# Routed experts with fp32r products in three terms instead of full-precision products

## The reference, cut to what matters

```python
def _ffn(x, w1, w2, w3):
    return jax.nn.silu(x @ w1.T) * (x @ w3.T) @ w2.T
for i in range(sw1.shape[0]):                 # 2 shared experts, over all 2048 rows
    shared = shared + _ffn(xf, sw1[i], sw2[i], sw3[i])
rw, sel = jax.lax.top_k(xf @ router_w.T + expert_bias, 2)
...
acc = acc + cw[:, None] * _ffn(xf, e1, e2, e3)   # 8 routed experts, 2 of them for a row
```

## Time and profile before

| | us |
|---|---|
| three runs, median (lowest to highest) | 3079.29 (3074.86 to 3079.81) |
| the profiled execution's own time | 3077.15 |
| its span, first to last instruction | 3075.1 |
| TensorE busy in the span | 2908.1 (95%) |
| VectorE, ScalarE, GpSimd busy | 1944.8, 1541.3, 1436.4 |
| stage of the 39 routed slots (2752 to 2975) | 223 |
| from there to the end | 100 |

### The profile page before, as it was taken

How to read it: one execution, slowest core, us unless ns; L and a number is a source line. 1 busy time by engine, 2 the same in 40 slices (tenths; PEclk the granted TensorE clock), 3 DMA queues, 4 the chain that set the end, 5 groups by cost and what they waited for, 6 DMA issues and landing times. The chain is left out here.

```text
span 3075.1 us, 35137 instructions
## 1 busy us (share of the span) xinstructions
PE 2908.1 (95%) x11882; PEld 1882.5 (61%) x11882; DVE 1944.8 (63%) x3365; ACT 1541.3 (50%) x2656; POOL 1436.4 (47%) x1122
## 2 busy tenths in 40 slices
PE   7577999999999999999999999999999999889997
PEld 3234565656665656565656566666777776676666
DVE  5896777775658676756776876566555554442226
ACT  5753545453545454536454544356777878311111
POOL 4495767660017575600376754004665757212213
PEclk9798999999999999999999999999999999799998
DMA  6352212111122121211211212011010100511112
GB/s 237 146 178 94 86 35 59 35 52 57 39 69 66 30 64 35 66 36 39 76 59 35 71 31 87 15 39 37 17 46 15 39 15 15 171 62 54 52 43 69
DMA packets 71685, 189.90 MB, mean 62 GB/s; under 512 B 8420, under 2 KB 39272, under 8 KB 63448
## 3 DMA queue, kind: packets, MB, share of 16 engines
q1 hardware_dynamic: 67096, 172.08, 18.3%
q0 software_dynamic: 3984, 15.60, 1.5%
q10 hardware_dynamic: 432, 0.01, 0.0%
HBM read 124.59 MB, written 28.44 MB: 50 GB/s over the span
## 5 line engine op out<-in xcount | busy, mean ns | idle before, releaser
L1131 ACT ACTIVATE a_carry<-a_st 128x512 f32<-128x512 f32 (+1 forms) x1088 | 649.1, 597 | 918.3 <-PE a_st L1567 905.4
L1587 PE MATMUL a_o<-a_carry,a_vals 128*65 128x512 f32 (+1 forms) x1632 | 835.6, 593 | 0.0
L1316 DVE TENSOR_REDUCE a_maxes<-a_mx 128x1 f32<-128x512 f32 x1016 | 677.5, 686 | 191.6 <-PE a_mx L1490 183.8
L949 POOL TENSOR_TENSOR a_plow<-a_carry,a_phigh 128x512 fp32r<-128x512 f32 (+1 forms) x272 | 349.1, 1291 | 259.5 <-ACT a_phigh L1134 255.9
L1567 PE MATMUL a_st<-a_q,a_kone 65*128 65x512 f32 (+1 forms) x1088 | 431.7, 397 | 0.0
L979 POOL TENSOR_TENSOR a_shared<-a_shared,a_bc 128x512 f32<-128x512 f32 x192 | 251.9, 1312 | 384.4 <-DVE a_shared L1251 384.4
L1251 DVE TENSOR_TENSOR_SCAN a_shared<-a_shared 128x512 f32<-128x512 f32 x192 | 289.0, 1508 | 14.1 <-POOL a_shared L968 12.7
L1566 PE MATMUL a_st<-a_q,a_keven 128*128 128x512 f32 (+1 forms) x544 | 296.0, 544 | 1.2 <-ACT a_q L1108 0.9
L1566 PE MATMUL a_st<-a_q,a_kodd 128*128 128x512 f32 (+1 forms) x544 | 286.8, 527 | 0.0
L1490 PE MATMUL a_mx<-a_kodd,a_q 128*128 128x512 f32 x512 | 275.7, 554 | 9.8 <-DVE a_maxes L1316 8.5
L1567 PEld LDWEIGHTS a_st<-a_q,a_kone 65*128 65x128 f32 (+1 forms) x1088 | 201.9, 186 | 123.7 <-issue 93.2
(11 more groups left out here) (278 smaller groups left out, 4948.4 us busy)
## 6 DMA issues: line engine op xcount, KB each, us to landing
a_bc<-m_kept_bc SPq DMA_DIRECT2D x48, 512.0 KB, 3.6
a_wt<-a_w_split SPq DMA_DIRECT2D x15, 1536.0 KB, 8.9
a_kone<-a_keven SPq DMA_DIRECT2D x32, 528.5 KB, 4.5
a_kone<-a_kodd SPq DMA_DIRECT2D x32, 528.5 KB, 4.3
e_wall<-in_w_t_dram SPq DMA_DIRECT2D x27, 512.0 KB, 5.5
a_shared<-m_kept_bc SPq DMA_DIRECT2D x16, 512.0 KB, 3.7
a_w_split<-a_wt POOLq DMA_DIRECT2D x4, 1536.0 KB, 5.4
a_shared<-in_ctx_dram SPq DMA_DIRECT2D x4, 1536.0 KB
```

Source lines behind the costliest of these rows:

```text
L949: nc.gpsimd.tensor_tensor(p_low(s)[0:r], p_of(s % 4)[0:r], p_high(s)[0:r].bitcast(F32), ALU.subtract).then_inc(p_low_ready, 1)
L1131: nc.scalar.activation(p_of(s % 4)[0:r], st[0:r, s % 2], ACT.Exp, scale=SCALE).then_inc(exp_done, 1)
L1316: nc.vector.reduce_max(maxes[:, c, t:t + 1], mx_bank(g, i), AX_X).then_inc(mx_max, 1)
L1587: nc.tensor.matmul(ps_o[0:DH + 1, g % 2], vals[0:r, kt * HG + j, :], p_of(s % 4)[0:r], start=(kt == 0), stop=(kt == KT - 1)).then_inc(pv_d ...
```

## The change

The routed slots get the three-term fp32r products that the shared experts have. The tables of a slot's owner are split slot by slot into the same `wh` and `wl`, which hold one slot's tables at a time:

- ScalarE makes the high parts, in two halves of 512 columns for each of the three tables (`split_parts` for w1 and w3, `split_down` for w2). It waits until TensorE has finished with the previous content: `first_used` and `h_done` for w1 and w3, `y_done` for w2.
- VectorE makes the low part of the first half of each table (`split_low`, `split_down_low`), GpSimd that of the second half.
- The turned rows and the turned gate are split too: `xh_col` and `xl_col` on VectorE, `gh_col` on ScalarE and `gl_col` on VectorE.
- TensorE has 12 products in `hidden_chosen` and 12 in `down_chosen`, at fixed addresses; the register load of the owner moves from TensorE to ScalarE, VectorE and GpSimd, one in each for a slot.
- The second shared expert goes through the same functions as a slot number 39 (`s == SLOTS`). Its w1 and w3 are loaded early, to `raw` and to the memory of `equal`; its w2 is loaded to `raw` after the last y row is stored. `split_next` is gone.

Core of the diff:

```diff
-            for j in range(SLOTS):
-                if j >= XR:
-                    pool.wait_ge(x_turned, j - XR + 1)
...
-                if j in (8, 16, 24):
-                    split_next((8, 16, 24).index(j))
+            def split_low(s, i):
+
+                pool.wait_ge(part_high, 4 * s + 2 * i + 2)
+                full = wall_of(own[s], i, 512, 1024) if s < SLOTS else shared_raw[i][:, 512:1024]
+                nc.gpsimd.tensor_tensor(wl[i][:, 512:1024], full, wh[i][:, 512:1024].bitcast(F32),
+                                        ALU.subtract).then_inc(part_low_pool, 1)
+            def split_down_low(s):
+                pool.wait_ge(down_high, 2 * s + 2)
...
+            for j in range(-1, SLOTS + 2):
+                if j + 1 < SLOTS:
+                    own[j + 1] = pool.value_load(owner[0:1, j + 1:j + 2], min_val=0, max_val=E - 1)
+                if j >= 2:
+                    split_down_low(j - 2)
+                if j < SLOTS:
+                    for i in range(2):
+                        split_low(j + 1, i)
+                if j == SLOTS + 1:
+                    split_down_low(SLOTS)
+                if 0 <= j < SLOTS - XR:
+                    fetch_x(j + XR)
```

ScalarE:

```diff
+            def split_parts(s):
+
+                if s < SLOTS:
+                    own[s] = act.value_load(owner[0:1, s:s + 1], min_val=0, max_val=E - 1)
+                for i in range(2):
+                    if s == 0 or i == 1:
+                        act.wait_ge(h_done, U0 + s)
+                    else:
+                        act.wait_ge(first_used, s)
+                    if s == SLOTS:
+                        act.wait_ge(raw_loaded[i], 16)
+                    for h in range(2):
+                        half_of = slice(512 * h, 512 * (h + 1))
+                        full = wall_of(own[s], i, 512 * h, 512 * (h + 1)) if s < SLOTS else shared_raw[i][:, half_of]
+                        nc.scalar.activation(wh[i][:, half_of], full, ACT.Copy).then_inc(part_high, 1)
...
             for j in range(SLOTS):
+                if j >= 2:
+                    split_down(j - 2)
+                split_parts(j + 1)
                 activate(U0 + j)
                 if j >= 1:
                     read_g(j - 1)
```

TensorE and SP:

```diff
+                for part in range(2):
+                    terms = [(x, w, k) for x, w in ((xh_col, wh[part]), (xl_col, wh[part]), (xh_col, wl[part])) for k in range(KD)]
+                    pe.wait_ge(part_high, 4 * j + 2 * part + 2)
+                    for i, (x, w, k) in enumerate(terms):
+                        if i == 4:
+                            pe.wait_ge(part_low_dve, 2 * j + part + 1)
+                        if i == 5:
+                            pe.wait_ge(part_low_pool, 2 * j + part + 1)
...
+                terms = [(g, w, m) for g, w in ((gh_col, wh[2]), (gl_col, wh[2]), (gh_col, wl[2])) for m in range(MT)]
+                for i, (g, w, m) in enumerate(terms):
+                    if i == 2 * MT:
+                        pe.wait_ge(down_low_dve, j + 1)
+                    if i == 2 * MT + 2:
+                        pe.wait_ge(down_low_pool, j + 1)
...
+            sp.wait_ge(part_low_dve, 2 * SLOTS + 1)
+            sp.wait_ge(part_low_pool, 2 * SLOTS + 1)
+            sp.dma_start(raw[:].rearrange("p (k n) -> p k n", n=cols[2]), by_rows(tables[2], E + 1)).then_inc(raw_loaded[2], 16)
```

More of the change, by code:

```diff
@@ L1702, in experts @@
         first_loaded = [sem(f"e_first_loaded{j}") for j in range(3)]
-        raw_loaded = sem("e_raw_loaded")
+        raw_loaded = [sem(f"e_raw_loaded{i}") for i in range(3)]
         w_high = sem("e_w_high")
@@ L1818, in _ @@
                                              bass.IndirectOffsetOnAxis(index[:, j:j + 1], 0)).then_inc(x_fetched[j % XR], 16)
-                if j in (8, 16, 24):
-                    split_next((8, 16, 24).index(j))
+            own = {}
+            for j in range(XR):
+                fetch_x(j)
+            for j in range(-1, SLOTS + 2):
[10 more added lines that the diff above has]
+                    fetch_x(j + XR)
             for r in range(2):
@@ L1879, in _, with split_down @@
                         gate_high(n, m - 1)
+            own = {}
+            def split_parts(s):
[12 more added lines that the diff above has]
+                        nc.scalar.activation(wh[i][:, half_of], full, ACT.Copy).then_inc(part_high, 1)
+            def split_down(s):
+                if s == 0:
+                    act.wait_ge(o_done, B * TT)
+                else:
+                    act.wait_ge(y_done, s)
+                if s == SLOTS:
+                    act.wait_ge(raw_loaded[2], 16)
+                for h in range(2):
+                    half_of = slice(512 * h, 512 * (h + 1))
+                    full = wall_of(own[s], 2, 512 * h, 512 * (h + 1)) if s < SLOTS else shared_raw[2][:, half_of]
+                    nc.scalar.activation(wh[2][:, half_of], full, ACT.Copy).then_inc(down_high, 1)
+            act.wait_ge(owner_ready, 1)
+            act.wait_ge(wall_loaded, 16 * 3 * E)
+            split_parts(0)
             for j in range(SLOTS):
+                if j >= 2:
+                    split_down(j - 2)
+                split_parts(j + 1)
                 activate(U0 + j)
@@ L2086, in _ @@
                         nc.vector.tensor_copy(index[:], ids).then_inc(index_ready, 1)
+                if n == B - 1:
+                    dve.wait_ge(owner_ready, 1)
+                    own[0] = dve.value_load(owner[0:1, 0:1], min_val=0, max_val=E - 1)
+                    for i in range(2):
+                        split_low(0, i)
                 add_dense(n)
-            read_x(0)
-            for j in range(SLOTS):
+            for j in range(-1, SLOTS + 1):
                 if j + 1 < SLOTS:
                     read_x(j + 1)
-                gate_on(U0 + j)
-                if j >= 2:
-                    read_y(j - 2)
+                if 0 <= j < SLOTS - 1:
+                    own[j + 1] = dve.value_load(owner[0:1, j + 1:j + 2], min_val=0, max_val=E - 1)
+                if j >= 1:
+                    gate_on(U0 + j - 1)
+                if j >= 3:
+                    read_y(j - 3)
+                if j >= 2:
+                    split_down_low(j - 2)
+                if 0 <= j < SLOTS:
+                    for i in range(2):
+                        split_low(j + 1, i)
+                if j >= 1:
+                    read_g_low(j - 1)
             for n in range(B, 2 * B):
@@ L2100, in _ @@
                         read_y(SLOTS - 2 + m)
+                    if n == B and m < 2:
+                        split_down_low(SLOTS - 1 + m)
                     if m > 0:
@@ L2197, in turn_x, with hidden_chosen @@
                 mm.then_inc(x_turned, 1)
[L2199 to L2202 removed]
+            def hidden_chosen(j):
                 u = U0 + j
@@ L2206, in hidden_chosen @@
                 for part in range(2):
-                    for k in range(KD):
-                        mm = nc.tensor.matmul(ps_h[:, u % 2, part], x_col[:, j % 2, k * P:(k + 1) * P],
-                                              table(e, part, k * HID, (k + 1) * HID), start=(k == 0), stop=(k == KD - 1))
-                mm.then_inc(h_done, 1)
+                    terms = [(x, w, k) for x, w in ((xh_col, wh[part]), (xl_col, wh[part]), (xh_col, wl[part])) for k in range(KD)]
[5 more added lines that the diff above has]
+                            pe.wait_ge(part_low_pool, 2 * j + part + 1)
+                        mm = nc.tensor.matmul(ps_h[:, u % 2, part], x[:, j % 2, k * P:(k + 1) * P],
+                                              w[:, k * HID:(k + 1) * HID], start=(i == 0), stop=(i == len(terms) - 1))
+                    mm.then_inc(h_done if part else first_used, 1)
             def turn_g(j):
@@ L2264, in _ @@
                     turn_x(j + 1)
-                own[j] = pe.value_load(owner[0:1, j:j + 1], min_val=0, max_val=E - 1)
-                hidden_chosen(j, own[j])
+                hidden_chosen(j)
                 if j >= 1:
```

94 lines of the change are left out of this document (63 added, 31 removed).

## The result

| | before | after |
|---|---|---|
| median of 11 executions, us | 3077.81 (3074.86 to 3079.81) | 3111.44 (3085.68 to 3115.78) |
| profiled execution, us (span) | 3077.15 (3075.1) | 3112.87 (3111.1) |
| fp32r products per slot | 0 | 24 |
| step from slot to slot, steady part, us | 5.82 | 6.35 and 6.72 in turn, mean 6.54 |

The kernel is slower: ratio of the mean times 1.0078, 95% interval 1.0061 to 1.0095. The executions after fall into two groups, five at 3085.7 to 3093.0 and six at 3111.4 to 3115.8; those of before into one. All profiles of the changed kernel are of the later group, so what follows explains that one. The mean granted clock is 0.975 to 0.977 in all eleven, so the clock does not make the groups.

What follows compares the result with a forecast made beforehand. TensorE was taken to bound the kernel before, GpSimd after, at 6.1 us per slot. Profiled 3077.15 + 10.9 (39 x 0.28) + 5.2 for start and end = 3093.3; the median lies 2.1 higher, so 3095, range 3062 to 3124.

Steps and rivals of the forecast that it cites:

- the likeliest case: Whole kernel: 5.85 to 6.45 us per slot, a time of 3086 to 3110 us; chance 0.40.
- TensorE, 4.81 a slot: Routed slots: TensorE's own work with the fp32r products takes 4.81 us, 1.01 less than before.
- ScalarE, 4.4: Routed slots: six added copies and the two earlier instructions take 4.4 us, full but under TensorE's 4.81.
- The load, 0.6 on VectorE, up to 1.0 on GpSimd: Owner's register load in each slot: taken as 0.6 us on VectorE, 0 to 1.0 on GpSimd.
- The collision: Routed slots: GpSimd's and VectorE's two-operand subtractions take turns; one turn per slot, costing GpSimd 0.60 us.
- The loop of 6.67: Slot chain through VectorE's subtraction, TensorE's products, two copies and GpSimd's subtraction: 6.67 us, possibly alternating with shorter slots.
- Start +0.8: Start of the routed stage: VectorE's load and two subtractions come first, TensorE's load goes; 0.8 us longer.
- End +4.4: After the slots: gathers start 5.0 us later behind the shared third table's subtraction, down products 0.6 shorter; +4.4 us.
- GpSimd keeps ahead: Faster rival: turns vanish in idle time, load hidden, slot 5.04 to 5.5 us, time 3066; chance 0.25.
- The clock: Slower rival: TensorE's granted clock falls; at 0.70 the slot is 6.9 us and the time 3126; chance 0.06.
- The loads in full: Slower rival: register loads paid in full, GpSimd 6.64 us per slot, time 3116; chance 0.17.
- The sign named for a wrong mechanism: Profile after: GpSimd idle waiting for ScalarE's copies in most slots, or no subtraction stretched, would refute the mechanism.

Runs made afterwards that it cites:

- experiment 7: Changed kernel with GpSimd making only 8 of its 512 columns of each low part in the slots; 3054.15 us, ratio 0.9919.
- Experiment 2: Changed kernel with fixed slot owners, so no register loads or address arithmetic on ScalarE, VectorE and GpSimd; median 3105.27 us.
- experiment 6: Changed kernel with VectorE making only 8 of its 512 columns of each low part in the slots; 3078.35 us.
- the second profile: Changed kernel as it is, profiled once more; that execution took 3115.35 us.
- experiment 5: Changed kernel with the low part of the shared expert's third table made whole by VectorE, slots unchanged; median 3112.51 us.
- experiment 8: Changed kernel with the third table's low part made whole by VectorE, in the slots and for the shared expert; median 3107.53 us, ratio 1.0095.
- experiment 3: Changed kernel with only hidden products in fp32r, down product in full precision, shared third table split in slot 6; median 3065.40 us, ratio 0.9957.
- experiment 10: Kernel of experiment 3 with VectorE's and TensorE's work reordered at the start of the stage; median 3061.05 us, ratio 0.9945.
- experiment 11: Kernel of experiment 10 with VectorE making both hidden tables' low parts whole, GpSimd splitting nothing in the slots; median 3056.99 us, ratio 0.9933.
- experiment 4: Changed kernel with GpSimd's row fetch moved between the third table's subtraction and the other two; median 3123.33 us, ratio 1.0152.
- experiment 1: Changed kernel with VectorE's table low parts as table times two numbers per partition; eight executions 3072.4 to 3074.2, two 3091.2 and 3091.5; ratio 0.9992.

## Why the prediction came out as it did

The direction, the range and the engine pair were right; the time of 3095 lies between the two groups and 16 below the median, which is also just above the likeliest case of 3086 to 3110. That the range held is in part luck, since the largest cost, VectorE's waiting, stands in it at nothing. By its steps:

- **TensorE, 4.81 a slot.** Right. Twelve hidden products take 2.77 and twelve down products 1.44; with GpSimd's share out (experiment 7) the step is 4.93.
- **ScalarE, 4.4.** Right: 108.11 of 160 us are 4.4 us in each step of 6.54, and the copies wait for TensorE, not the other way round.
- **The load, 0.6 on VectorE, up to 1.0 on GpSimd.** Too high. VectorE shows 0.29 of idle behind it (7.3 us in 25 times, put down to issue); on GpSimd it lies under other work. Experiment 2: 0.18 a slot for all loads.
- **The collision.** This is the step that failed. The prediction let GpSimd pay it, "one such turn in a slot, 0.60", and put it on VectorE at nothing ("VectorE: 4.9 us without any collision"). GpSimd's part was about right: 48 x (1521 - 1291) ns and 25 x (1240 - 968) ns, the unstretched means being those of experiments 6 and 7, are 17.8 us in 25 slots, 0.71 each. VectorE's was not there at all: 50 x (1210 - 681) and 25 x (1683 - 689) ns are 51.3 us, **2.05 a slot**. VectorE's own 4.26, the 0.29 and 2.05 make 6.60, beside a step of 6.54: VectorE, which waits for no other engine's result there, became the bound through waiting for its turn. The term was priced by the turn that GpSimd gives away (0.60); the turn that VectorE gives away is one or two of GpSimd's subtractions, 1.27 or 2.5.
- **The loop of 6.67.** Not the loop that the trace shows, so its nearness to the long slot's 6.72 is luck. The chain of waits does not pass through two copies and GpSimd's subtraction, but through VectorE's, at 2.45 and not at 0.60; with 2.5 as its first link the forecast's loop would come to 8.6. The short slot is not shorter by much (6.35), where the forecast averaged down to 6.1. So 39 x 0.28 = 10.9 became 28.5.
- **Start +0.8, measured +1.3** by the first gate. The terms as the prediction names them, 1.0 + 2 x 0.60 - 1.0, add up to 1.2 and not to 0.8; the two profiles of the changed kernel differ by 2.7 there, so no finer statement is possible.
- **End +4.4, measured +6.2** (+6.8 in the second profile). The gathers start 13.8 behind the last gate instead of 9.3, so 4.6 later where 5.0 was forecast, and the chain of waits passes through them. That this "shows in the end in full" was wrong: experiment 5 took GpSimd's part away and got 1.7 to 2.3, experiment 8 nothing; in both, TensorE's wait for the table, which "lies beside it", has taken its place in the chain of waits. Where the shared table is loaded early (experiments 3, 10 and 11) this part is 100.6, 99.0 and 99.1. So 3 to 5 us of it go with the late load, felt on both engines; these kernels have another down product too, so the figure is an estimate.
- **Rivals.** "GpSimd keeps ahead" fell with the stretched rows. The clock did not fall: 1.00 in the steady part, with TensorE at 79%; only the first slots had less, 0.91 in 2752 to 2790. The loads in full were not paid. The sign named for a wrong mechanism ("if GpSimd shows idle time waiting for ScalarE's copies in most slots") half came true: 18.4 us in 13 waits, every second slot, which should be read as GpSimd not being the bound.

Shown by experiments: without GpSimd's share nothing is stretched and the step is 4.93 (7), less work on GpSimd does not give the time back as long as VectorE still meets it (8), the loads are not it (2). Argued from the rows only: the split of the step into 4.26, 0.29 and 2.05. Open: what the end would cost without the late load, and why some executions take 25 us less.

## What to carry to other kernels

When work is shared between VectorE and GpSimd and both read on-chip memory, price the collision on both engines: VectorE's instruction can stand for two of GpSimd's (2.5 us here), however short it is itself. Look in the trace at the same line's shortest and longest instance, and at VectorE's twins with an operand in PSUM, which are the undisturbed measure. Before a third engine is brought in, work out whether the two can do it alone: here VectorE alone fed the hidden products at 5.12 us a slot with no idle time on TensorE, and the part that did not fit (the down product, 0.3 a slot) was better left undone.

## What the runs showed of the hardware

- A waiting VectorE subtraction is not always next. At 2865.92 it stood until GpSimd's second subtraction had ended; in the kernel without VectorE's share, one of 8 columns that started at 2866.26, in the last 0.19 of a GpSimd subtraction, stood through the next two as well and took 2.69. Nor does the earlier one always go first: in experiment 4 VectorE's of 2864.72 (the one before it ended at 2864.80) took 3.36, while GpSimd's pair began only at 2864.97. At 2872.31 and 2872.86 in the changed kernel the two engines alternated. What decides between these was not found. The Trainium skill (SBUF — State Buffer, "Who interferes with whom") says that the one that issues first has the shared pair for its whole instruction and the other blocks fully; that explains a wait for one instruction, not the one for two, nor the case of 2864.72.
- GpSimd's indirect DMA took 1.24 us in each of 25 cases of the changed kernel. In every one a VectorE subtraction with two on-chip operands was still running when it began, and ran on for 0.4 us. Where none was running at its start it took 0.97, 30 times of 30 in the kernel without GpSimd's share, and also 10 times in experiment 4, where such a subtraction started 0.06 us or more behind the DMA and ran beside it. In experiment 4's other 13 cases one was running, and the DMA took 1.24. In experiment 1, where VectorE's instruction ended 0.12 to 0.14 into the DMA, it took 0.97. So what costs the 0.27 is a subtraction that runs on into the DMA's start. The same section of the Trainium skill holds that a two-operand VectorE instruction does not disturb the making of descriptors, and marks this as inferred; the 0.27 speaks against it for this case, the 10 cases of experiment 4 speak for it.
- In the kernel of experiment 3 the granted clock fell to 0.50 (the 1.2 GHz level) in the first slots, behind waits of TensorE of 1.52 and 1.07 us that ended at 2754.20 and 2755.68. The stretches at either level (us, busy times, clock in the column behind GpSimd's):

```profile
2758.40:2760.40 2.00, 2.00 (x6) 1.62 (x5) 0.69 (x1) 1.15 (x2) 0.37 (x1) 0.50 0.19 56
...
2776.20:2778.00 1.80, 1.80 (x12) 1.55 (x11) 1.23 (x3) 1.59 (x4) 0.66 (x1) 1.00 0.47 142
```

  Two matmuls of 512 columns take 0.85 from start to start at the lower level (2758.36 to 2759.21) and 0.45 at the upper (2776.16 to 2776.61). Whether the waits caused the fall is not shown: the second execution of the changed kernel had waits of 1.52 and 1.06 in the same place, and its clock was 1.00 from 2757 to 2763; there it fell to 0.68 in 2766 to 2770, behind a wait of 1.61 for fetched rows.
